# Cross attention with undivided exponentials, split float32r scores, and every block move issued by SyncE

## The reference

```
q = query @ Wq.T + bq;  k = ctx @ Wk.T + bk;  v = ctx @ Wv.T + bv       # 16 heads of 32
scores = einsum('bqhd,bkhd->bhqk', q / sqrt(32), k)                     # 100 x 722 for each head
probs  = softmax(scores, axis=-1)
attn   = einsum('bhqk,bkhd->bqhd', probs, v)
x = layernorm(x + attn @ Wo.T + bo)
```

## Time and profile before

| | us |
|---|---|
| median of 3 runs | 2386.76 (2382.62 to 2387.44) |
| the profiled execution | 2381.39, its span 2379.6 |
| first to last start of a move of D | 524.6 to 1894.8 |
| PE busy | 2330.8 (98% of the span) |
| DVE, ACT, POOL busy | 1510.4, 1347.2, 1399.3 |

### The profile page before, as it was taken

The page is one execution under the profiler, slowest core; times in us unless marked ns, Lnnn a source line. Parts: engine busy times, 40 slices in busy tenths (PEclk is TensorE's granted clock), DMA queues, the critical chain, the costliest instruction groups (busy, mean ns, idle before and its releaser), DMA issues.

```text
span 2379.6 us, 58683 instructions
## 1 busy us (share of the span) xinstructions
PE 2330.8 (98%) x21642; PEld 2033.3 (85%) x21642; DVE 1510.4 (63%) x2563; ACT 1347.2 (57%) x3322; POOL 1399.3 (59%) x1211
## 2 busy tenths in 40 slices
PE   8999989999999999999999999999999899999999
PEld 7888758988888888888888888888888699998998
DVE  4676788836767677676767677676766734435342
ACT  5888852236666666666666666666666642231321
POOL 4777677347667667667666667667665533333332
PEclk9999979999999999999999999999999999999999
DMA  7444478537777777777677777777677831101000
GB/s 190 131 130 120 118 205 321 212 100 195 185 198 199 204 188 203 192 200 208 178 207 193 198 197 197 196 197 204 179 201 198 253 133 36 50 18 66 7 33 24
DMA packets 254825, 384.60 MB, mean 162 GB/s; under 512 B 116760, under 2 KB 132184, under 8 KB 254552
## 3 DMA queue, kind: packets, MB, share of 16 engines
q1 hardware_dynamic: 229976, 330.65, 49.4%
q10 hardware_dynamic: 24576, 50.36, 8.3%
HBM read 126.33 MB, written 40.60 MB: 70 GB/s over the span
## 4 chain that ended last, share of the span: by engine, by line
PE 75%; DVE 1%; issue 1%; ACT 1%; ACTq 0%; POOL 0%; DVEq 0%; POOLq 0%
PE D_ps_p L69 42%; PE D_ps_s L1995 7%; PE D_ps_p L2022 6%; PE E_ps_g L69 6%; PE E_ps_u L69 6%; PE E_ps_d L69 5%; PE E_ps_y L69 3%; ACT D_e L1650 1%; DVE D_columns L1792 0%; PE E_ps_t L2051 0%; ACTq L1666 0%; DVE D_turned L1806 0%; DVE E_stats_a L1849 0%; DVE E_r_a L1865 0%; ACT D_values L1639 0%
## 5 line engine op out<-in xcount | busy, mean ns | idle before, releaser
L1511 POOL TENSOR_SCALAR D_e<-D_e,D_columns 128x722 f32<-128x722 f32 x256 | 538.5, 2103 | 438.1 <-DVE D_columns L1798 437.8
L1792 DVE TENSOR_REDUCE D_columns<-D_ps_s 128x1 f32<-128x723 f32 x512 | 439.7, 899 | 350.2 <-PE D_ps_s L1995 350.0
L1650 ACT ACTIVATE D_e<-D_ps_s,D_columns 128x723 f32<-128x723 f32 x512 | 436.9, 861 | 238.5 <-DVE D_columns L1792 238.5
L1806 DVE STREAM_TRANSPOSE D_turned<-D_e 128x768 f32<-128x768 f32 x512 | 495.5, 972 | 21.1 <-DMA D_pT<-D_turned 20.3
L69 PE MATMUL D_ps_p<-D_ctx_high,cross_wk_high 128*128 128x384 f32 (+1 forms) x1024 | 346.0, 338 | 2.9 <-DVEq L1818 1.5
L69 PE MATMUL D_ps_p<-D_ctx_low,cross_wk_high 128*128 128x384 f32 (+1 forms) x1024 | 333.2, 325 | 0.0
L69 PE MATMUL D_ps_p<-D_ctx_high,cross_wk_low 128*128 128x384 f32 (+1 forms) x1024 | 333.0, 325 | 0.0
L1657 ACT ACTIVATE D_e<-D_e,D_columns 128x722 f32<-128x722 f32 x256 | 230.2, 899 | 59.8 <-DVE D_columns L1798 59.8
L69 PE MATMUL D_ps_p<-cross_wv_high,D_ctx_low 128*128 128x512 f32 (+1 forms) x656 | 257.9, 393 | 0.0
L69 PE MATMUL D_ps_p<-cross_wv_low,D_ctx_high 128*128 128x512 f32 (+1 forms) x656 | 257.7, 393 | 0.0
L69 PE MATMUL D_ps_p<-cross_wv_high,D_ctx_high 128*128 128x512 f32 (+1 forms) x656 | 255.8, 390 | 0.7 <-ACT D_values L1639 0.7
(11 more groups left out here) (264 smaller groups left out, 5225.6 us busy)
## 6 DMA issues: line engine op xcount, KB each, us to landing
D_pT<-D_turned SPq DMA_DIRECT2D x1536, 96.0 KB, 2.7
D_pT<-D_turned ACTq DMA_DIRECT2D x512, 96.0 KB, 2.9
D_craw<-in_ctxT SPq DMA_DIRECT2D x124, 361.0 KB, 4.2
self_v<-wstage SPq DMA_DIRECT2D x25, 256.0 KB, 2.6
A_v<-self_v SPq DMA_DIRECT2D x32, 200.0 KB
self_o<-A_o SPq DMA_DIRECT2D x32, 200.0 KB, 4.1
x<-C_x SPq DMA_DIRECT2D x5, 1280.0 KB, 5.8
cross_q<-C_qo SPq DMA_DIRECT2D x20, 320.0 KB, 4.1
```

Source lines behind the costliest of these rows:

```text
L1511: pool.tensor_scalar(head, head, inv[:, 2 * (s % 2):2 * (s % 2) + 1], None, ALU.mult)\
L1650: act.activation(e[n // 2 % 2][:, n % 2, 0:PARTS * PART].rearrange("p (a c) -> p a c", a=PARTS), parts_of(n), ACT.Exp, bias=neg_max[:, n % ...
L1792: dve.tensor_reduce(neg_max[:, n % 4:n % 4 + 1], parts_of(n), AX.XY, ALU.max, negate=True)\
L1806: dve.transpose(turned[quad % 2][:, :, 2 * (s % 2) + h, :].rearrange("p j (t r) -> p t j r", r=32), e[s % 2][:, h, :].rearrange("p (t j r) ...
```

## The change

Exponentials are turned as they come out of `exps`. The row sums of a quad are turned too (`turn_sums`), and their reciprocals (`inverses`) are written into unused columns of `turned` (`inverse_of`: 5 of the 7 columns between two blocks of 25 queries), so that the moves of the quad carry them to `pT`. `take_result` multiplies the weighted sum by them. Both divisions of the exponentials and the single reciprocals go. The bias of the values becomes an operation of POOL on the result (`add_values_bias`).

Scores become three float32r products of a high and a low part of queries and keys, 36 matmuls of 242 or 238 columns. The low part of the keys is made by DVE from the PSUM bank (`low_keys`), that of the queries by POOL. Keys and queries of two quads are kept in place of those of a batch; keys are projected two steps ahead of their scores, and a key's bank is free when `low_keys` has read it. Queries are loaded once for each quad, with four DMAs for a batch in place of one.

`move` issues all 16 DMAs of a quad on SP, and also waits for `inv_done` and for the scaled result of the quad two before; ACT issues none. The lists of ACT and DVE are written by quads.

```diff
-        ks = rest("D_keys", [P, QUADS, S])
-        qraw = rest("D_qraw", [P, QUADS, T])
+        both_keys = rest("D_keys", [P, 4, S], F32R)
+        ks = [both_keys[:, 2 * part:2 * part + 2, :] for part in range(2)]
+        qraw = rest("D_qraw", [P, 2, T])
...
-                unit_at.setdefault(PAIRS * (b - 1) + u + 2, []).append(("k", b, u))
+                unit_at.setdefault(PAIRS * b + u - KEYS_AHEAD, []).append(("k", b, u))
...
             if kind == "k":
-                pe.wait_ge(k_done, KU * b + n + 1)
+                pe.wait_ge(k_low, KU * b + n + 1)
...
                 def move(quad):
                     sp.wait_ge(turn_done, 4 * quad + 4)
-                    wait(sp, pv_done, quad - 1)
-                    for d in range(1, BLOCKS):
+                    sp.wait_ge(inv_done, quad + 1)
+                    wait(sp, scaled, quad - 1)
+                    for d in range(BLOCKS):
                         for a in (0, 2, 1, 3):
                             j = (a + d) % BLOCKS
                             sp.dma_start(pT[quad % 2][32 * j:32 * (j + 1), a, :, :],
...
                 for b in range(B - 1):
-                    load_q(b + 1)
                     if b > 0:
                         move(QUADS * b - 1)
+                    load_q(QUADS * b + 3)
...
-                def normalise_second(s):
...
-                def move_diagonal(s):
...
+                def quad_at(s):
                     if s >= 0:
                         exps(2 * s)
                         exps(2 * s + 1)
+                    take_units("k", s)
+                    if s >= 0:
+                        exps(2 * s + 2)
+                        exps(2 * s + 3)
+                    take_units("k", s + 1)
+                    take_units("v", s)
+                    take_units("v", s + 1)
...
+                def turn_sums(quad):
+                    dve.wait_ge(exp_done, 4 * quad + 4)
+                    wait(dve, inv_done, quad)
+                    dve.transpose(sums, rowsum.unsqueeze(2).broadcast_to([P, BLOCKS, 32])).then_inc(sums_turned, 1)
+
+                def inverses(quad):
+                    dve.wait_ge(sums_turned, quad + 1)
+                    dve.wait_ge(turn_done, 4 * quad + 1)
+                    dve.reciprocal(inverse_of(turned[quad % 2]),
+                                   sums[:, :, 0:QB].rearrange("p j (t c) -> p j t c", c=GAP)).then_inc(inv_done, 1)
...
-                    dve.tensor_scalar(oo[b % 2][:, m, :], bank("o", quad, 0)[:, 0:T], bv_c[:, m:m + 1], None, ALU.add)\
-                       .then_inc(o_done, 1)
+                    dve.tensor_tensor(oo[b % 2][:, m, :].rearrange("p (a t c) -> p a t c", a=BLOCKS, c=GAP),
+                                      bank("o", quad, 0)[:, 0:T].rearrange("p (a t c) -> p a t c", a=BLOCKS, c=GAP),
+                                      inverse_of(pT[quad % 2]), ALU.mult).then_inc(scaled, 1)
...
+                            dve.scalar_tensor_tensor(ks[1][:, m % 2, first:end], bank("k", b, u)[:, 0:end - first],
+                                                     bk_c[:, m:m + 1], ks[0][:, m % 2, first:end].bitcast(F32),
+                                                     ALU.add, ALU.subtract).then_inc(k_low, 1)
...
+                        for n, (q, k) in enumerate(SPLIT):
+                            for j in range(4):
+                                rows = slice(HD * j, HD * (j + 1))
+                                last = pe.matmul(of_head[:, j, a, 0:end - first],
+                                                 qs[q][rows, quad % 2, :, :].rearrange("p a q -> p (a q)"),
+                                                 ks[k][rows, quad % 2, first:end],
```

More of the change, by code:

```diff
@@ L1132, in phase_cross_and_feed_forward @@
         oo = [rest(f"D_o{i}", [P, QUADS, T]) for i in range(2)]
-        columns = rest("D_columns", [P, 5, 4])
-        bk_c, bv_c, neg_max, rowsum, inv = (columns[:, n, :] for n in range(5))
+        columns = rest("D_columns", [P, 4, 4])
+        bk_c, bv_c, neg_max, rowsum = (columns[:, n, :] for n in range(4))
         even = Region(even_at, odd_at)
@@ L1426, in _ @@
                 load_q(0)
+                load_q(1)
                 load_ctx(1, 2)
@@ L1588, in _ @@
                     pool.memset(vs[i][:, ST - 1, :], 0.0).then_inc(consts, 1)
-                pool.memset(qs[:, :, :, :], 0.0).then_inc(consts, 1)
-                pool.wait_ge(consts, 8)
+                for part in range(2):
+                    pool.memset(qs[part][:, :, :, :].bitcast(F32), 0.0).then_inc(consts, 1)
+                pool.wait_ge(consts, 9)
                 pool.wait_ge(all_max, 1)
@@ L1608, in _ @@
                     add_bias(0, i)
[L1609 removed]
+                add_values_bias(last - 4)
                 rstd_of("a", 0)
[L1611 removed]
                 add_bias(0, 3)
[L1613 to L1617 removed]
+                for i in range(1, 4):
+                    rstd_of("a", i)
                 add_bias(0, 4)
@@ L1629, in take_keys @@
                     act.wait_ge(u_done, unit_count["k", b, u])
-                    wait(act, s_done, QUADS * (b - 1) + m + 1)
-                    act.activation(ks[:, m, first:end], bank("k", b, u)[:, 0:end - first], ACT.Identity,
-                                   bias=bk_c[:, m:m + 1]).then_inc(k_done, 1)
+                    wait(act, s_done, QUADS * b + m - 1)
+                    act.activation(ks[0][:, m % 2, first:end], bank("k", b, u)[:, 0:end - first], ACT.Identity,
+                                   bias=bk_c[:, m:m + 1]).then_inc(k_high, 1)
                 def take_values(b, i):
@@ L1752, in _ @@
                                 high_of(acts, acts_raw, first_loaded[(n - KD) // 2], n - KD, o_high)
-                step(MAIN)
-                step(MAIN + 1)
+                for s in range(FIRST, MAIN, 2):
+                    quad_at(s)
+                    first_highs(s)
+                    first_highs(s + 1)
+                quad_at(MAIN)
                 def with_weights(tile):
@@ L1986, in scores, with part @@
                     if quad == 0:
[L1987 to L1989 removed]
+                        pe.wait_ge(consts, 9)
+                    pe.wait_ge(q_low, quad + 1)
+                    pe.wait_ge(k_low, KU * b + 2 * m + 2)
                     wait(pe, exp_done, 4 * quad)
[L1992 removed]
+                    def part(a, passed_by=()):
                         first, end = a * PART, min(a * PART + PART, S)
[L1994 to L2004 removed]
+                        for n, (q, k) in enumerate(SPLIT):
[4 more added lines that the diff above has]
+                                                 ks[k][rows, quad % 2, first:end],
+                                                 start=(n == 0), stop=(n == len(SPLIT) - 1), tile_position=(HD * j, 0))
+                                if n == len(SPLIT) - 1 and j in passed_by:
+                                    last.then_inc(left_bank, 1)
+                        return last
+                    part(0, passed_by=(1, 3))
+                    part(1)
                     pe.wait_ge(left_bank, 2 * (quad + 1))
[L2007 to L2009 removed]
+                    part(2).then_inc(s_done, 1)
                 def weighted_sum(quad):
```

244 lines of the change are left out of this document (113 added, 131 removed).

## The result

The changed kernel takes **2662.4 us** (median, 2657.5 to 2665.7), the kernel before in the same session 2385.5 us (2382.6 to 2387.4): a ratio of **1.116**, 95% interval 1.1138 to 1.1182. The prediction was 2647 us in 2570 to 2700. The profiled execution has a span of 2655.7 us.

What follows compares the result with a forecast made beforehand. PE bound the kernel before; after the change SP's queue of DMAs would. Before the moves 524.6, issuing 1621, waits 15, after the moves 484.6: 2645 us of span, +1.8 around it, 2647 us; range 2570 to 2700.

Steps and rivals of the forecast that it cites:

- SP's price and count: SP's queue between first and last move: 2416 DMAs at 0.671 us each, 1621 us, setting the pace; chance 0.78.
- issuing gets cheaper when ACT issues none: Rival on SP's queue: 0.55 to 0.60 us for each of 2416 DMAs, 2420 to 2570 us; chance 0.07.
- SP's waits: SP's queue during the moves: 15 us of waiting in all, between 0 and 60.
- The loop: From a move's landing through turn, low keys, value units, scores, maxima and scaling: 10.5 or 13.3 us, within SP's 14.6.
- The sum and its range: Whole kernel: 524.6 + 1621 + 15 + 484.6 = 2645 us of span, 2647 with 1.8 around it; range 2570 to 2700.
- PE waits for low keys, 250 to 350 us: Sign in the trace after: PE waits in its value units for DVE's low keys, some 250 to 350 us in all.
- The rival of the clock: Rival on PE: its clock falls in its waits, +40 to +120 us, 2690 to 2770; chance 0.08.
- PE's scores, 1.43 us to 0.9 to 1.25: PE's scores of each quad: some 0.3 us less, 38 us if PE were the bound, here idle time.
- DVE, POOL, ACT: DVE at some 9.4 us of 12.7 a quad, not the bound; 538.5 and 230.2 us of POOL's and ACT's divisions worth nothing.
- Ends: Before the first move and after the last: 524.6 and 484.6 us, kept as they were, the first within 5 us.
- The two pages: Skill pages on issuing: one makes moving 512 DMAs cost nothing (PE decides, 2343 or 2381 us, chance 0.03), the other opposes it.

## Why the prediction was right, step by step

- **SP's price and count.** 2416 DMAs at 0.671 us were to take 1621 us; they took 1593 (0.659). The count was exact. Four of the five rows above with 2064 DMAs or more lie at 0.653 to 0.667, the fifth at 0.684. Why those two of the kernel before with ACT issuing lie highest (0.671, 0.684) is open; ACT issuing four or six of them gives 0.665 and 0.658 in the changed kernel. The rival "issuing gets cheaper when ACT issues none" has at most that 0.01 to 0.02 us in it.
- **SP's waits.** 15 us were given, 0 to 60 as bounds; 58.7 came. This is the term that was mis-sized. The loop was counted with a value unit at 2.85 us; behind a wait it took 5.2 at 1.2 GHz, so 13.3 us for the loop with two units become some 15.7 by this estimate, more than the 14.6 available. That the loop then closes late shows in SP's 22 waits for D_o (40.3 us), each behind a stretch at 1.2 GHz; with other order on VectorE 3.4 us were left.
- **The sum and its range.** The span came out 10 us over the 2645 of the sum, and part of that is luck: the price was 28 us too high, the waits 44 us too low and the ends 5 us too high. The upper bound also doesn't follow from its own terms: 0.69 us for each of 2416 DMAs and 60 us of waits give 2738, not 2700. The measured time lies inside either way.
- **PE waits for low keys, 250 to 350 us.** 198.5 us. PE was idle for 209 us of the stretch in all (1651.8 less 1443.1); its busy time, which was to fall, rose from 1359 to 1443 us, since 181 us of the stage ran at 1.2 GHz; its share of the span is 90%, not 87. The rival of the clock was right in that the clock fell and that the loop then closed late, and too high in its worth (40 to 120 us): it could cost only through SP's waits for D_o, 40 us, and those need the order on VectorE too. The argument against it, that PE stays busy over 80%, didn't help: that is a mean over the stage (87%, 1443 of 1652 us), and the clock fell in single waits such as the one of 4.5 us.
- **PE's scores, 1.43 us to 0.9 to 1.25.** 36 records from 1009.60 to 1010.85, 1.25 us: the slow end. They were forecast to be worth nothing behind a full SP. That was measured with four moves on ACT (nothing), not in the changed kernel itself, whose SP has even less to spare. Where TensorE binds they are worth 22 us, 0.17 a quad; I had 38, since I took 0.3 us.
- **DVE, POOL, ACT.** 768.7 us of divisions went from POOL and ACT and no experiment shows them on the path. A sharper form of it is the kernel with four moves on ACT: all of the change but the 512 moves, and 52 us slower than before, not faster. That had no place in my prediction: 45 us of it came from where SP's store stands; then two more moves on ACT gave 8 us and the place of the low halves another 10.
- **Ends.** 520.6 and 483.3 us against 524.6 and 484.6, together 5 us less than given. 520.6 + 1593 + 58.7 + 483.3 is the span.
- **The two pages.** The Trainium skill, "DMA: Bandwidth & Descriptors" (Issuing engines are not separate DMA queues), says that the sequencer's time is usually small relative to the DMA. Here an issue takes 0.59 us and its DMA lands after 2.2, but many are in flight, so the landings overlap and the issues, one every 0.66 us, add up: the time saved by a second issuing engine was not small. The Trainium skill, "Perfetto Trace Analysis" (DMA Optimizations), advises to balance DMAs over the engines that can issue them where an engine is busy with issuing. The runs agree: four of sixteen given back to ACT were worth 225 us.

## What to carry to other kernels

Give each queue that issues DMAs a share of the span of its own, from (DMAs) x (start to start) plus its waits, before anything is put on it; the page of shares doesn't list it, and in stage D of the kernel before it stood at 89% behind a PE at 99%. Count the waits in such a queue as occupation too: a store that waits 2 us ahead of twelve moves cost 45 us, and moving it cost nothing. What an edit is worth has to be measured where its engine binds: the same edit of the scores gave 0 us under one bound and 22 under the other.

## What the runs showed of the hardware

- The time for which an issue of a move holds SyncE doesn't depend on its bytes: 96 KB and 48 KB for each give medians of 592 and 591 ns, with the DMA engines at 0.65 and at 0.39. It does differ between kinds of DMA: in the timelines above a context load of 361 KB holds the queue for 0.44 us, a query load of 50 KB for 0.58. The 0.66 us are the mean of this mix.
- Neither does it depend much on a second issuing engine: 592 ns with ACT issuing none, 593 to 594 with ACT issuing 512 or 768.
- Issues far over the median come in every kernel (maxima 1863 to 2243 ns), with half the bytes too; in the changed kernel 95 of the 2048 moves take over 900 ns. What they wait for isn't known; they lift the mean from 0.63 us (the median with the gap) to 0.66.
- Behind a wait of 4.5 us without matmuls TensorE ran at 1.2 GHz for the next 5 us (granted clock 0.52); 181 us of the stage ran so by the record of the granted clock, and nothing of it in the kernel before.
